# One loop over 64 graphs for four graph layers, with the directed layers taken upper, lower, single in a round

## The chip, the cores and the metric

The kernel runs on one core of one Trainium2 chip. The metric is the device time of one execution in microseconds. A core has TensorE (PE), VectorE (DVE), ScalarE (ACT), GpSimd (POOL) and SyncE (SP), which here issues all DMAs. Each engine runs its own list of instructions in order, and they meet at semaphores.

## The reference

For each of 64 independent graphs of 128 nodes, x is 128 x 384 and adj is 128 x 128. Four layers follow, each with a norm and a relu ahead of it and a residual sum behind it:

```python
h = relu(layernorm(x)); x = x + L0(h, adj)   # attention, 12 heads of 32, masked where adj is 0
h = relu(layernorm(x)); x = x + L1(h, adj)   # one directed layer
h = relu(layernorm(x)); x = x + L2(h, adj)   # two directed layers, the second on the output of the first
h = relu(layernorm(x)); x = x + L3(h, adj)   # attention, 12 heads, adj added to the scores, and an output projection
# a directed layer:
attn = softmax(h h^T / sqrt(D)) * adj;  attn = attn / (row sum + 1e-10)
ctx = upper(attn) @ (h Wl + bl) + diag(attn) * (h Ws + bs) + lower(attn) @ (h Wr + br)
out = relu(layernorm(ctx) * gain + offset)
```

To keep precision with 16-bit products, each operand of a product is held as a high and a low half in fp16 (hi, lo), and each product is three matmuls (`three_products`, L147).

## The kernel before

The kernel runs four phases one after the other. x of all 64 graphs stays in SBUF between them. `attention` (L347) serves L0 and L3, `directed` (L923) serves L1 and L2; in L2 the tasks of the first and the second directed layer of neighbouring graphs alternate. Within a phase a software pipeline is written out by hand in `step`: on each engine the list of operations of one task, each for the graph that is k tasks ahead or behind. `Phase.run` (L103) and `TwoLayerPhase.run` (L129) repeat it. Between two phases the engines meet, the next layer's weights are scaled, turned by TensorE where needed and split into halves by ScalarE and VectorE (`find_scales` L264, `split_high` L292, `split_low` L285, `turn` L301). Their loads and part of the search for their largest value (`largest`, L231) are done in the phase before.

In attention a task is: norm (`norm` L479, `normed` L534), turn h on TensorE (`turn_h` L798) and split it (`turned_hi` L540, `turned_lo` L650), project q and k (`project_turned` L807) and v (`project_v` L819), scores (`score` L829), the bias added and the row maximum found by VectorE, four heads at a time (`biased_max` L655), exponentials by ScalarE into f32 (`exponents` L545). TensorE then turns the f32 probabilities, 12 tiles of 128 x 128 (`turn_probs` L838), ScalarE takes the high half out of PSUM (`p_split` L570, the instruction at L572) and VectorE the low half (`p_split` L689, instruction at L692), and TensorE multiplies by v (`attend` L844). In L3 the result is turned (`turn_o` L855) and projected (`project_out` L862); GpSimd sums the scores to find rows that are all zero (`fold_scores` L501).

In a directed task TensorE computes h h^T (`similarity` L1294), the left, right and own projection (`project` L1301), turns the masked exponentials (L1311) and combines (L1335 to L1338, the last of these products waits for `right_lo` of GpSimd). VectorE has the row maximum, mask, diagonal, the sums with biases (`biased` L1197), the low half of the left values (`left_lo` L1193, instruction at L1195), `context` (L1202) and its statistics. GpSimd computes the power for the norm and the product behind it (`ctx_norm` L999, instructions L1003 and L1005), the low halves of the sides and of the right values (L1009, L1014), gain and offset (L1016, L1021). ScalarE has the exponential, the high halves, `norm_ctx` (L1088, instruction L1091) and `weighted_own` (L1081).

PSUM has eight banks. L0 and L3 use all of them, the directed phases seven.

## Time and profile before

| | us |
|---|---|
| median of 3 runs (lowest, highest) | 2752.17 (2751.03, 2753.88) |
| the profiled execution | 2754.08 |
| its span, first to last instruction | 2752.5 |
| TensorE busy | 2520.6, 92% |
| VectorE busy | 2336.4, 85% |
| ScalarE busy | 1804.1, 66% |
| GpSimd busy | 1453.0, 53% |
| DMA, mean over the span | 60.19 MB, 22 GB/s |
| mean granted clock of TensorE, as a share of full speed | 0.979 |

In 40 slices of 68.8 us, busy tenths, with the clock below them (9 is 90% or more):

```profile
PE   5999999986999999699999999999969999999998
...
DVE  5778777776999999688888888888859999999997
...
PEclk9999999997999999799999999999979999999998
```

The first nine slices are L0, the next seven L1, then thirteen of L2, and the last eleven L3; the dips are the changes of phase. Busy times of matmuls overlap, since a product's modelled end lies beyond the start of its successor: what a product costs is read from start to start.

### The profile page before, as it was taken

To read this page: it belongs to the slowest core of one execution; us is meant where nothing else is said; L and a number is where in the kernel's file an instruction comes from. 1 tells how busy PE (TensorE), PEld (TensorE's weight loads), DVE (VectorE), ACT (ScalarE), POOL (GpSimd) and SP (SyncE) were. 2 spreads that over 40 slices of the span, in tenths; PEclk is the share of its full clock that TensorE was granted. 3 is DMA by queue.
4 is the path that set the end of the run, shared out by engine and by line. 5 is a ranking of instruction groups with operands and counts; after the bars stand their busy time and mean duration, and the time that the engine had idled before them with its cause. 6 is when DMAs were issued, how large, how long until landed. Compare 5 with 4: busy or idle time off the path is not lost. (4 is left out here: it accounts for less than half of the span.)

```text
span 2752.5 us, 86859 instructions
## 1 busy us (share of the span) xinstructions
PE 2520.6 (92%) x27969; PEld 1884.4 (68%) x27969; DVE 2336.4 (85%) x9515; ACT 1804.1 (66%) x4409; POOL 1453.0 (53%) x2016
## 2 busy tenths in 40 slices
PE   5999999986999999699999999999969999999998
PEld 4888888874666665466666666666648888888886
DVE  5778777776999999688888888888859999999997
ACT  5888888874555555455555555555538777777775
POOL 1233232324777777477777777777734434444443
PEclk9999999997999999799999999999979999999998
DMA  3011010102000000100000000000000000000000
GB/s 105 28 30 29 28 30 27 30 14 88 9 9 10 10 10 9 46 10 10 10 10 10 10 10 10 10 10 10 10 6 22 24 25 23 27 23 27 23 27 23
DMA packets 73988, 60.19 MB, mean 22 GB/s; under 512 B 7888, under 2 KB 73936, under 8 KB 73936
## 3 DMA queue, kind: packets, MB, share of 16 engines
q1 hardware_dynamic: 73936, 59.54, 7.1%
q8 instruction: 27, 0.44, 0.1%
q14 instruction: 25, 0.20, 0.0%
HBM read 46.92 MB, written 12.58 MB: 22 GB/s over the span
## 5 line engine op out<-in xcount | busy, mean ns | idle before, releaser
L149 PE MATMUL bank<-L_w_hi,L_hT_hi 128*128 128x384 f16 x2112 | 691.7, 327 | 0.0
L151 PE MATMUL bank<-L_w_hi,L_hT_lo 128*128 128x384 f16 x2112 | 691.5, 327 | 0.0
L150 PE MATMUL bank<-L_w_lo,L_hT_hi 128*128 128x384 f16 x2112 | 691.4, 327 | 0.0
L550 ACT ACTIVATE raw_weights<-L_minus_scores,L_minus_max 128x128 f32<-128x128 f32 x1536 | 476.0, 389 | 69.5 <-DVE L_minus_max L665 67.7
L149 PE MATMUL bank<-L_hT_hi,L_w_hi 128*128 128x128 f16 x2304 | 413.4, 220 | 1.7 <-issue 1.2
L150 PE MATMUL bank<-L_hT_lo,L_w_hi 128*128 128x128 f16 x2304 | 413.3, 220 | 0.0
L151 PE MATMUL bank<-L_hT_hi,L_w_lo 128*128 128x128 f16 x2304 | 413.2, 220 | 0.0
L665 DVE CUSTOM_DVE_ANT_0 L_minus_scores<-bank,L_minus_score_bias 128x128 f32<-128x128 f32 x1536 | 347.8, 282 | 11.4 <-PE bank L834 5.9
L692 DVE TENSOR_TENSOR L_pT_lo<-bank,L_pT_hi 128x512 f16<-128x512 f32 x384 | 241.0, 682 | 126.6 <-ACT L_pT_hi L572 126.5
L1069 ACT ACTIVATE L_e<-bank,L_nmax 128x128 f32<-128x128 f32 x192 | 70.6, 368 | 365.6 <-DVE L_nmax L1154 365.6
L151 PEld LDWEIGHTS bank<-L_w_hi,L_hT_lo 128*128 128x128 f16 x2112 | 207.5, 98 | 138.2 <-issue 2.5
L483 POOL TENSOR_TENSOR L_ln_scale_bias<-L_var_eps,minus_half 128x1 f32<-128x1 f32 x128 | 70.5, 551 | 403.0 <-DVE L_var_eps L631 397.1
L150 PEld LDWEIGHTS bank<-L_w_lo,L_hT_hi 128*128 128x128 f16 x2112 | 207.5, 98 | 108.5 <-issue 2.2
L149 PEld LDWEIGHTS bank<-L_w_hi,L_hT_hi 128*128 128x128 f16 x2112 | 207.9, 98 | 98.7 <-issue 1.7
L491 POOL TENSOR_TENSOR L_xsum<-L_attended,L_bias_v 128x384 f32<-128x384 f32 x64 | 64.1, 1001 | 385.8 <-DVE L_attended L713 385.8
L1014 POOL TENSOR_TENSOR L_right_lo<-L_right,L_right_hi 128x384 f16<-128x384 f32 x192 | 211.3, 1101 | 75.6 <-ACT L_right_hi L1075 74.9
L1003 POOL TENSOR_TENSOR L_cln_scale_bias<-L_cvar_eps,minus_half 128x1 f32<-128x1 f32 x192 | 106.1, 552 | 235.1 <-DVE L_cvar_eps L1222 235.1
L149 PEld LDWEIGHTS bank<-L_hT_hi,L_w_hi 128*128 128x128 f16 x2304 | 227.1, 99 | 2.7 <-issue 2.5
L150 PEld LDWEIGHTS bank<-L_hT_lo,L_w_hi 128*128 128x128 f16 x2304 | 227.1, 99 | 0.7
L572 ACT ACTIVATE L_pT_hi<-bank 128x512 f16<-128x512 f32 x384 | 201.0, 596 | 40.4 <-PE bank L841 40.4
L151 PEld LDWEIGHTS bank<-L_hT_hi,L_w_lo 128*128 128x128 f16 x2304 | 227.1, 99 | 0.0
L1029 POOL TENSOR_TENSOR L_ob<-L_og,L_gain_offset_biases 128x384 f32<-128x384 f32 x192 | 191.4, 997 | 20.1 <-POOL L_og L1019 9.8
(165 smaller groups left out, 7531.3 us busy)
## 6 DMA issues: line engine op xcount, KB each, us to landing
adj_tile<-in_adj SPq DMA_DIRECT2D x320, 64.0 KB, 1.8
x<-in_x SPq DMA_DIRECT2D x64, 192.0 KB, 2.3
out<-L_result SPq DMA_DIRECT2D x64, 192.0 KB, 1.9
raw_weights<-in_L_gnn_Wq SPq DMA_DIRECT2D x2, 576.0 KB, 4.0
raw_weights<-in_L_gnn_Wk SPq DMA_DIRECT2D x2, 576.0 KB, 5.7
raw_weights<-in_L_gnn_Wv SPq DMA_DIRECT2D x2, 576.0 KB, 5.5
raw_weights<-in_L_gnn_Wl SPq DMA_DIRECT2D x2, 576.0 KB, 4.9
raw_weights<-in_L_gnn_Ws SPq DMA_DIRECT2D x2, 576.0 KB, 4.8
```

Of the source, the lines that this page charges most:

```text
L149: pe.matmul(out, stat[0], move[0], start=first, stop=False)
L150: pe.matmul(out, stat[0], move[1], start=False, stop=False)
L151: return pe.matmul(out, stat[1], move[0], start=False, stop=last)
L483: pool.tensor_tensor(ln[:, 0:1], ve[:, 0:1], minus_half[:, :], ALU.pow).then_inc(rstd_ready, 1)
L550: last = act.activation(probs[:, n_.slot(k), i, :], scores[:, i, :], ACT.Exp, bias=nmax[:, n_.slot(k), i:i + 1], scale=-1.0)
L572: act.activation(pT[0][:, HC * c:HC * c + HC, :], pT_banks[c][:, :].rearrange("p (h q) -> p h q", h=HC), ACT.Copy).then_inc(pT_hi[c], 1)
L665: last = dve.tensor_tensor_reduce(scores[:, i, :], s_banks[j][:, c128(c)], bias[:, n_.slot(), :], 1.0, -LOWEST, ALU.add, ALU.min, nmax[:, ...
L692: dve.tensor_tensor(pT[1][:, hs, :], pT_banks[c][:, :].rearrange("p (h q) -> p h q", h=HC), pT[0][:, hs, :], ALU.subtract).then_inc(pT_lo[ ...
L1003: pool.tensor_tensor(cln[:, 0:1], cve[:, 0:1], minus_half[:, :], ALU.pow).then_inc(d["crstd_ready"], 1)
L1014: pool.tensor_tensor(rightv[1][:, :], right[:, :], rightv[0][:, :], ALU.subtract).then_inc(d["r_lo"], 1)
L1029: pool.tensor_tensor(ob[:, :], og[:, :], tables[n_.kind(k)][1], ALU.add).then_inc(d["tail_ready"], 1)
L1069: act.activation(e[:, :], u_bank[:, 0:P], ACT.Exp, bias=nmax[:, 0:1], scale=scalev, accum_out=zsum[:, :]).then_inc(d["p_ready"], 1)
```

## The change

The four phases become one loop over rounds (`run_rounds`). A round holds one task of each of five kinds: `first` (L0), `single` (L1), `lower` and `upper` (first and second layer of L2) and `last` (L3), each for its own graph. A step is given as kind and lag: `n_.last(2)` in round n works on graph n - 2. `Order` says in which sequence tasks that share buffers follow each other: `first` and `last` share those of attention, and the directed kinds follow as upper, lower, single. x is kept for two graphs at each of four places (x0 to x3) and no longer for all. All weights live in SBUF at once; W0 is prepared first, and W1, W2 and W3 in a block before round 0 (`more_weights`), W2 and W3 loaded into the room that the raw W0 and W1 had, with three PSUM banks for turning instead of six. That room later holds f32 scratch tiles.

The probabilities are split in SBUF (`probs_hi` on ScalarE, `probs_lo` on VectorE) into `p16`, and a DMA turns both halves of four heads at once (`turn_probs` on SP, 128 x 1024 fp16, 256 KB); TensorE no longer turns them. All f32 transposes of h, of the masked exponentials and of the attended rows remain. The similarity, the masked exponentials and the turned h of a directed task now share one PSUM bank, left and right another, own and context a third; q, k, v, the turned h and the scores of attention share four, and the product with v, the turned attended rows and the output have the eighth bank. The arithmetic of each operation is unchanged. The core of the diff, with the indentation of nested functions taken off; the step lists of SP and ScalarE are left out:

```diff
+ATTENTION = Order(("first", 0), ("last", 2))
+DIRECTED = Order(("upper", 2), ("lower", 1), ("single", 0))
+NORMED = tuple(kind for kind in DIRECTED.kinds if kind != "upper")
+FIRST_ROUND, LAST_ROUND = -3, G - 1 + 4
+LOOP = (4 + 4) // 2 * 2, (G - 1 + -3) // 2 * 2
...
+def run_rounds(eng, step, before_round):
+
+    for n in range(FIRST_ROUND, LOOP[0]):
+        if n in before_round:
+            before_round[n](eng)
+        step(Round(eng, n))
+    with eng.Fori(LOOP[0] // 2, LOOP[1] // 2) as i:
+        values = {"i": i, "from": LOOP[0] // 2}
+        for s in (0, 1):
+            step(Round(eng, (2, s), values))
+    for n in range(LOOP[1], LAST_ROUND + 1):
+        step(Round(eng, n))
 
 
...
-                        def turn_probs(n_, k, c):
-                            wait(pe, probs_ready[c], n_.done(k))
-                            for j in range(HC):
-                                mm = pe.transpose(pT_banks[c][:, c128(j)], probs[:, n_.slot(k), HC * c + j, :], ident[:, :])
-                            mm.then_inc(pT_psum[c], 1)
...
+        dhT_bank, u_bank, e_bank = banks[0], banks[0], banks[0]
+        l_bank, r_bank = banks[1], banks[1]
+        own_bank, c_bank = banks[2], banks[2]
+        pv = banks[3][:, 0:H * (HD + 1)].rearrange("p (h e) -> p h e", h=H)
+        oT_bank, o_bank = banks[3], banks[3]
+        hT_bank, q_bank, k_bank, v_bank = banks[4], banks[5], banks[6], banks[7]
...
+def turn_probs(t, c):
+    if t is None:
+        return
+    wait_apart(sp, (pT_ready[c], t.count(-1, 16)), (p_lo[c], t.count()), (pv_psum, t.count(-1)))
+    sp.dma_start_transpose(pT[:, c, :, :],
+                           p16[:, c, :, :, :].rearrange("p a h n -> p (a h n)")).then_inc(pT_ready[c], 16)
...
+def more_weights(eng):
+    W0.ready(sp)
+    W1.ready(sp)
+    W2.load(sp)
+    W2.ready(sp)
+    W3.load(sp)
+    W3.ready(sp)
+
+load_x(Task(sp, ATTENTION, "first", 0, None))
+W0.load(sp)
+W1.load(sp)
+run_rounds(sp, step, {0: more_weights})
+sp.wait_ge(out_written, 16 * G)
+
+            @block.gpsimd
...
+def step(n_):
+    dir_norm(n_.single(0))
+    right_lo(n_.lower(1))
+    att_norm(n_.first(-1))
+    add_v_bias(n_.first(-1))
+    add_out_bias(n_.last(2))
+    fold_scores(n_.last(2))
+    context_norm(n_.lower(1))
+    fold_again(n_.last(2))
+    gain(n_.lower(1))
+    offset(n_.lower(1))
+    sides_lo(n_.single(0))
+    right_lo(n_.single(0))
+    context_norm(n_.single(0))
+    gain(n_.single(0))
+    offset(n_.single(0))
+    sides_lo(n_.upper(1))
+    right_lo(n_.upper(1))
+    dir_norm(n_.lower(0))
+    context_norm(n_.upper(1))
+    gain(n_.upper(1))
+    offset(n_.upper(1))
+    att_norm(n_.last(1))
+    add_attended(n_.first(-1))
+    sides_lo(n_.lower(0))
...
+def probs_hi(t, c):
+    if t is None:
+        return
+    wait_apart(act, (probs_ready[c], t.count()), (pT_ready[c], t.count(-1, 16)))
+    act.activation(p16[:, c, 0, :, :], probs[:, HC * c:HC * c + HC, :], ACT.Copy).then_inc(p_hi[c], 1)
...
+def dir_input(t):
+    if t is None:
+        return
+    if t.kind == "upper":
+        wait(act, d["hT_psum"], t.count(-1))
+        wait(act, d["tail_ready"], Task(act, DIRECTED, "lower", t.graph, t.values).count())
+        act.activation(dh[:, :], ob[:, :], ACT.Relu).then_inc(d["h2_ready"], 1)
+    else:
+        wait_apart(act, (d["ln_ready"], t.count(of=NORMED)), (d["hT_psum"], t.count(-1)))
+        x = x1 if t.kind == "single" else x2
+        act.activation(dh[:, :], x[:, t.parity(), :], ACT.Relu, bias=dln[:, 1:2],
+                       scale=dln[:, 0:1]).then_inc(d["h_ready"], 1)
...
+def probs_lo(t, c):
+    if t is None:
+        return
+    wait(dve, p_hi[c], t.count())
+    dve.tensor_tensor(p16[:, c, 1, :, :], probs[:, HC * c:HC * c + HC, :], p16[:, c, 0, :, :],
+                      ALU.subtract).then_inc(p_lo[c], 1)
...
+def add_to_x(t):
+    if t is None:
+        return
+    if t.kind == "upper":
+        wait(dve, xsum_ready, t.graph_count(-2))
+    wait(dve, d["tail_ready"], t.count())
+    old, new, ready = (x1, x2, x2_ready) if t.kind == "single" else (x2, x3, x3_ready)
+    dve.scalar_tensor_tensor(out=new[:, t.parity(), :], in0=ob[:, :], scalar=0.0, in1=old[:, t.parity(), :],
+                             op0=ALU.max, op1=ALU.add).then_inc(ready, 1)
...
+def step(n_):
+    dir_stats(n_.single(0))
+    dir_mean_var(n_.single(0))
+    dir_var_eps(n_.single(0))
+    att_var_eps(n_.first(-1))
+    left_lo(n_.lower(1))
+    dir_turned_lo(n_.single(0))
+    biased_max(n_.last(2), 0)
+    biased_max(n_.last(2), 1)
+    biased_max(n_.last(2), 2)
+    row_max(n_.single(0))
+    minus_row_max(n_.single(0))
+    context(n_.lower(1))
+    context_stats(n_.lower(1))
+    scaled_eps(n_.lower(1))
+    context_mean_var(n_.lower(1))
+    context_var_eps(n_.lower(1))
+    left_sum(n_.single(0))
+    mask(n_.single(0))
+    att_turned_lo(n_.first(-1))
+    part_sides(n_.single(0))
+    diagonal(n_.single(0))
+    v_lo_split(n_.last(2))
+    right_sum(n_.single(0))
+    probs_lo(n_.last(2), 1)
+    score_sums(n_.last(2))
+    left_lo(n_.single(0))
+    score_bias(n_.first(-1))
+    nonzero_sums(n_.last(2))
+    dir_turned_lo(n_.upper(1))
+    denominator(n_.single(0))
+    probs_lo(n_.last(2), 0)
+    probs_lo(n_.last(2), 2)
+    context(n_.single(0))
+    scaled_denominator(n_.single(0))
+    context_stats(n_.single(0))
+    scaled_eps(n_.single(0))
+    context_mean_var(n_.single(0))
+    row_max(n_.upper(1))
+    context_var_eps(n_.single(0))
+    minus_row_max(n_.upper(1))
+    biased_max(n_.first(-1), 0)
+    mask(n_.upper(1))
+    kept_rows(n_.last(2))
+    diagonal(n_.upper(1))
+    left_sum(n_.upper(1))
+    biased_max(n_.first(-1), 1)
+    denominator(n_.upper(1))
+    left_lo(n_.upper(1))
+    part_sides(n_.upper(1))
+    biased_max(n_.first(-1), 2)
+    right_sum(n_.upper(1))
+    add_to_x(n_.single(0))
+    dir_stats(n_.lower(0))
+    scaled_denominator(n_.upper(1))
+    row_sums(n_.last(2))
+    dir_mean_var(n_.lower(0))
+    row_scales(n_.last(2))
+    probs_lo(n_.first(-1), 0)
+    dir_var_eps(n_.lower(0))
+    attended_rows(n_.last(2))
+    context(n_.upper(1))
+    scaled_eps(n_.upper(1))
+    context_stats(n_.upper(1))
+    probs_lo(n_.first(-1), 2)
+    context_mean_var(n_.upper(1))
+    context_var_eps(n_.upper(1))
+    dir_turned_lo(n_.lower(0))
+    probs_lo(n_.first(-1), 1)
+    row_max(n_.lower(0))
+    turned_o_lo(n_.last(2))
+    minus_row_max(n_.lower(0))
+    v_lo_split(n_.first(-1))
+    left_sum(n_.lower(0))
+    add_to_x(n_.upper(1))
+    att_stats(n_.last(1))
+    att_mean_var(n_.last(1))
+    att_var_eps(n_.last(1))
+    add_result(n_.last(2))
+    att_stats(n_.first(-2))
+    mask(n_.lower(0))
+    drop_masked(n_.first(-2))
+    diagonal(n_.lower(0))
+    row_sums(n_.first(-1))
+    denominator(n_.lower(0))
+    row_scales(n_.first(-1))
+    attended_rows(n_.first(-1))
+    att_mean_var(n_.first(-2))
+    att_turned_lo(n_.last(1))
+    part_sides(n_.lower(0))
+    scaled_denominator(n_.lower(0))
+    right_sum(n_.lower(0))
+    score_bias(n_.last(1))
...
+def combine(t):
+    if t is None:
+        return
+    wait(pe, d["a_lo"], t.count())
+    wait(pe, d["l_lo"], t.count())
+    wait(pe, d["own_ready"], t.count())
+    three_products(pe, c_bank[:, 0:D], (sidesv[0][:, 0, :], sidesv[1][:, 0, :]),
+                   (leftv[0][:, :], leftv[1][:, :]), first=True, last=False)
+    wait(pe, d["r_hi"], t.count())
+    pe.matmul(c_bank[:, 0:D], sidesv[0][:, 1, :], rightv[0][:, :], start=False, stop=False)
+    pe.matmul(c_bank[:, 0:D], sidesv[1][:, 1, :], rightv[0][:, :], start=False, stop=False)
+    wait(pe, d["r_lo"], t.count())
+    pe.matmul(c_bank[:, 0:D], sidesv[0][:, 1, :], rightv[1][:, :], start=False, stop=True)\
+        .then_inc(d["c_psum"], 1)
...
+def step(n_):
+    project_q(n_.last(2))
+    dir_turn_h(n_.single(0))
+    score(n_.last(2))
+    combine(n_.lower(1))
+    similarity(n_.single(0))
+    project_left(n_.single(0))
+    att_turn_h(n_.first(-1))
+    project_v(n_.last(2))
+    project_self(n_.single(0))
+    turn_e(n_.single(0))
+    project_right(n_.single(0))
+    project_q(n_.first(-1))
+    dir_turn_h(n_.upper(1))
+    project_k(n_.first(-1))
+    combine(n_.single(0))
+    similarity(n_.upper(1))
+    score(n_.first(-1))
+    project_left(n_.upper(1))
+    project_self(n_.upper(1))
+    turn_e(n_.upper(1))
+    project_right(n_.upper(1))
+    attend(n_.last(2), 0)
+    attend(n_.last(2), 1)
+    attend(n_.last(2), 2)
+    combine(n_.upper(1))
+    project_v(n_.first(-1))
+    dir_turn_h(n_.lower(0))
+    turn_o(n_.last(2))
+    similarity(n_.lower(0))
+    project_left(n_.lower(0))
+    project_out(n_.last(2))
+    project_right(n_.lower(0))
+    attend(n_.first(-1), 0)
+    attend(n_.first(-1), 1)
+    attend(n_.first(-1), 2)
+    turn_e(n_.lower(0))
+    att_turn_h(n_.last(1))
+    project_self(n_.lower(0))
+    project_k(n_.last(1))
...
+
+pe.wait_ge(setup, 2)
+W0.ready(pe)
+run_rounds(pe, step, {0: more_weights})
```

## Rows read from the trace of the kernel before

**Rows 1.** The page, part 1: busy us, share, instructions.

```profile
PE 2520.6 (92%) x27969; PEld 1884.4 (68%) x27969; DVE 2336.4 (85%) x9515; ACT 1804.1 (66%) x4409; POOL 1453.0 (53%) x2016
```

**Rows 2.** Busy by stretch: length, busy us (instructions), granted clock, DMA share, GB/s.

```profile
200.00:300.00 100.00, 92.78 (x1584) 83.98 (x1584) 78.34 (x419) 83.91 (x221) 30.21 (x44) 1.00 0.10 29
800.00:900.00 100.00, 98.03 (x680) 60.96 (x679) 92.69 (x346) 57.73 (x130) 74.42 (x115) 1.00 0.03 9
1400.00:1500.00 100.00, 98.22 (x694) 61.82 (x693) 86.64 (x317) 57.30 (x132) 72.83 (x103) 1.00 0.03 10
2000.00:2100.00 100.00, 72.29 (x790) 56.74 (x789) 67.86 (x259) 52.33 (x122) 37.31 (x48) 0.85 0.04 11
2300.00:2400.00 100.00, 93.08 (x1409) 80.83 (x1410) 95.73 (x410) 77.29 (x199) 41.82 (x48) 1.00 0.07 24
```

**Rows 3.** Timeline, TensorE, one L3 graph: start, us, line, tiles, count.

```profile
2300.58 0.55 PE L859 MATMUL bank<-identity,L_attended 128*128 128x128 f32 x3 [0.60 <-DVE L_attended L713]
...
2303.98 0.33 PE L149 MATMUL bank<-L_w_hi,L_oT_hi 128*128 128x384 f16 x1
...
2305.44 1.47 PE L841 MATMUL bank<-identity,raw_weights 128*128 128x128 f32 x12
...
2306.75 0.33 PE L149 MATMUL bank<-L_w_hi,L_hT_hi 128*128 128x384 f16 x1
...
2309.59 0.95 PE L834 MATMUL bank<-L_kT,L_qT 32*128 32x128 f32 x24
...
2311.33 0.54 PE L859 MATMUL bank<-identity,L_attended 128*128 128x128 f32 x3 [0.79 <-DVE L_attended L713]
```

**Rows 4.** Timeline, several engines, in L2.

```profile
1505.85 0.34 PE L1338 MATMUL bank<-L_right_lo,L_sides_hi 128*128 128x384 f16 x1
...
1506.29 0.56 DVE L1207 TENSOR_TENSOR L_ctx<-bank,L_own_weighted 128x384 f32<-128x384 f32 x1 [0.81 <-PE bank L1338]
...
1509.65 0.55 POOL L1003 TENSOR_TENSOR L_cln_scale_bias<-L_cvar_eps,minus_half 128x1 f32<-128x1 f32 x1 [1.74 <-DVE L_cvar_eps L1222]
...
1510.05 0.56 DVE L1200 TENSOR_TENSOR L_right<-bank,L_gain_offset_biases 128x384 f32<-128x384 f32 x1
...
1510.42 0.67 POOL L1009 TENSOR_TENSOR L_sides_lo<-L_sides,L_sides_hi 128x256 f16<-128x256 f32 x1
...
1510.50 0.71 ACT L1091 ACTIVATE L_o<-L_ctx,L_cln_scale_bias 128x384 f32<-128x384 f32 x1 [0.16 <-POOL L_cln_scale_bias L1005]
...
1510.52 0.98 DVE L1195 TENSOR_TENSOR L_left_lo<-L_left,L_left_hi 128x384 f16<-128x384 f32 x1
...
1511.50 0.55 DVE L1133 BATCH_NORM_STATS2 L_bn<-x 128x6 f32 x1
...
1512.14 0.18 DVE L1137 BATCH_NORM_AGGREGATE L_mean_var<-L_bn 128x2 f32<-128x6 f32 x1
```

**Rows 5.** A group on VectorE by form: busy us, mean ns, idle before.

```profile
L665 DVE CUSTOM_DVE_ANT_0 L_minus_scores<-bank,L_minus_score_bias 128x128 f32<-128x128 f32 x1536 | 347.8, 282 | 11.4 <-PE bank L834 5.9 <-issue 5.5
```

**Rows 6.** Two single lines: duration ns, least, median, most.

```profile
L1195 DVE TENSOR_TENSOR L_left_lo<-L_left,L_left_hi x192: 544/910/1045, 661.2 to 2023.0; 128x384 f16<-128x384 f32 x192
...
L1160 DVE CUSTOM_DVE_ANT_0 L_e_masked<-L_e,adj_tile x192: 291/291/294, 656.9 to 2020.6; 128x128 f32<-128x128 f32 x192
```

**Rows 7.** The page, part 6: DMA issues, KB each, us to landing.

```profile
x<-in_x SPq DMA_DIRECT2D x64, 192.0 KB, 2.3
...
raw_weights<-in_L_gnn_Wk SPq DMA_DIRECT2D x2, 576.0 KB, 5.7
```

**Rows 8.** One line: first and last start of the L0 projections.

```profile
L812 PE MATMUL bank<-ones_in_rows_and,L_bias_rows x384: 219/219/314, 31.0 to 608.6; 128*128 128x128 f16 x192
```

**Rows 9.** Timeline, VectorE, preparing weights of L1 and L2.

```profile
642.94 0.17 DVE L269 TENSOR_SCALAR pow<-gall 128x4 int32<-128x4 int32 x1 [5.21 <-POOL gall L280]
...
1125.44 9.54 DVE L289 SCALAR_TENSOR_TENSOR L_w_lo<-bank,weight_scale,L_w_hi 128x384 f16<-128x384 f32 x18
```

**Rows 10.** DMA rate in 40 slices of 640 to 700 us.

```profile
GB/s 0 0 0 5 0 0 0 0 0 0 74 343 388 274 392 161 0 39 132 390 387 266 244 311 356 70 18 25 0 5 0 46 3 0 0 0 44 0 0 0
```

2023 lines of the change are left out of this document (969 added, 1054 removed).

## Prediction

> **What bounds the kernel now.** I read the page's engine totals first, then busy time by stretch, then one graph on TensorE in order of time, then the helpers' durations. TensorE is busy 92% of the span [rows 1]; in the directed stages 98% at full clock, in L3 93% beside a VectorE at 96%, in L0 93% [rows 2]. So TensorE's own work sets three stages and VectorE shares L3; the rest is the space between stages, where a stretch of 100 us holds only 72 us of TensorE work at clock 0.85 [rows 2].
>
> Time per graph follows from instruction counts. An L0 graph is 144 records, so 1584 records in 100 us are 11 graphs, 9.09 us each. A directed task is 47: 680 and 694 give 6.91 (L1) and 6.77, over the stretches 6.80 (L2). An L3 graph runs from turn to turn, 10.75 us here, 10.63 on the mean of its stretch (1409 records of 150) [rows 2, 3]. One graph therefore costs 9.09 + 6.91 + 2 x 6.80 + 10.63 = 40.2 us. 64 of them are 2575 us; 177 us of the 2752.5 us span are the start, three changes of stage and the end.
>
> **Part 1: work moved.** Of an L3 graph 0.79 us is idle and 1.31 us is the 12 transposes of probabilities [rows 3], so TensorE keeps 10.75 - 0.79 - 1.31 = 8.65 us. L0 is that without turning and projecting the output (0.38 + 1.46) and with six bias products more (0.34): 7.15. A directed task is 9 x 0.056 (similarity) + 34 x 0.1625 (nine products take 1.46 us) [rows 3] + 0.45 of transposes = 6.48. A round holds one task of each kind: 7.15 + 8.65 + 3 x 6.48 = 35.2 us of TensorE against 40.2 now. That is the most the change can win: 5 us a round, of which 2.6 are transposes and the rest idle time.
>
> VectorE: 2336 us [rows 1] less some 60 for weights and starts is 35.6 us a graph. About 2.5 of that is blocking behind GpSimd (below), so 33.1 us of bare work. ScalarE has 27.6, GpSimd 22.6 by the same division. The splits of probabilities stay (six of 512 columns on each of two engines) but read SBUF, not PSUM; the nearest row, 384 columns from SBUF, takes at least 0.544 us [rows 6], so 512 cost about 0.68 unblocked, which is what the split costs now: no change.
>
> **Part 2: the order within a round.** TensorE has 35.2 us of work, VectorE 33 to 36. With both that full, every engine keeps a written order, and a chain that crosses engines is late wherever the next queue is behind. I follow the cycle that closes on itself from one round to the next, with handovers of the trace. (a) VectorE's stats of x1 for the single layer to its turn on TensorE: stats 0.64 to the aggregate, 0.25, 0.30, GpSimd's power and product 0.85 up to ScalarE's start, ScalarE 0.76: 2.8 [rows 4]. (b) From that turn TensorE's own work to the end of project_k(first) is 12.9: turns 3 x 0.34 and 0.11, score 0.95, combine 0.98, similarity 0.5, left, v and right 1.46 each, self 1.63, q and k of first 30 x 0.056 = 1.68 each; two short waits (the scaled q; the upper layer's input, behind ScalarE's third block of exponentials) add 0.2 and 0.5: 13.6. (c) combine(single) and the handover: 0.98 + 0.28 = 1.3 (VectorE starts 0.44 after the last product) [rows 4]. (d) VectorE from context(single) to dir_var_eps(lower): 7 operations of 384 columns that follow each other at 0.48 [rows 4], 3 blocks of score maxima at 0.86 (four heads of 0.21) [rows 5], one 512-column split 0.62, part_sides 0.36, two masks 0.46, row_max 0.28, some 14 tiny ones at 0.12: 9.4. (e) GpSimd 0.85, ScalarE 0.76 and its queue 0.25: 1.85. (f) Turn of the lower layer, its two halves evicted, up to similarity: 0.34 + 0.2 + 0.52 + 0.6 = 1.65. (g) TensorE to turn_e(lower): 0.5 + 3 x 1.46 + attend 1.05 (2.84 up to the scores less 1.46 and 0.33) [rows 3] + 0.11 = 6.05. (combine(upper) waits up to 1.8 us for right_lo, with project_v(first) and all of TensorE behind it, but the cycle through VectorE is later.) (h) Waiting 0.45 for the last layer's input (x3 comes from combine(upper) over nine handovers), then the turn and its two halves: 2.0. (i) VectorE's last four operations: 1.2. Unblocked sum 39.85.
>
> Blocking: one half-split starts at 1510.52 while GpSimd works from 1510.42 to 1511.09, and takes 0.98 instead of 0.544; the line's median is 0.910 [rows 4, 6]. The trace has no round in which GpSimd's order stands beside these operations, so its price has two ends: zero, and 0.5 for each of two such splits in (d), left_lo(upper) and probs_lo(first). I take the line's median excess, 0.37 each, 0.75: the period is 40.6 us.
>
> **Part 3: the DMA transposes.** Six a round, 256 KB each, from SP's queue; what is queued behind one is the next transposes, adjacency loads and the write. No transpose by DMA is in the trace. Nearest rows: a plain 192 KB lands in 2.3 us, 576 KB in 5.7 [rows 7], so 256 KB plain would be about 2.7. Between probs_lo(first, 1) and attend(first, 1) my round leaves 4.7 us, so up to there it is hidden; lower bound of its cost nothing, upper (three times the plain time) 3.3 us a round. I take nothing, the end the plain rows are nearest to. The Trainium skill, "DMA: Bandwidth & Descriptors", Latency and other measured facts, gives an effective 261 GB/s for a DMA transpose, an estimated 1.0 us for 256 KB on top of the fixed part; by that the sum stays, and no row here shows it.
>
> **Part 4: outside the full rounds.** All five tasks run in rounds 2 to 62, 61 rounds. Start: first L0 projection at 31 us [rows 8], 30 here (one x load less before the weights), then graph 0 alone through attention with latencies bare: about 22. Weights of W1, W2, W3 in one lump before round 0, nothing beside it: 16 reductions of 1.34 = 21; three scales, each with 5.2 us of waiting for GpSimd's maximum [rows 9] and 1.8 of small steps = 21; 39 splits, now at 0.53 each (9.54 for 18) [rows 9], with three banks for six about 0.67 = 26; loads of W2 and W3 bare, 5.5 and 2.8 MB at the 350 to 390 GB/s of such loads [rows 10] plus fixed parts = 26; bias rows, first pieces and the value bias 9: 103. Rounds 0 and 1 are half empty but bound by the chain: 31 and 35. Rounds 63, 64, 65 and the last write: 34 + 31 + 22 = 87. Together 30 + 22 + 103 + 31 + 35 + 87 = 308 us, where the kernel before has 177. TensorE idles in the lump; the clock after it is the 0.85 kind of stretch, at most 10 us and in those numbers.
>
> **Sum.** 308 + 61 x 40.6 = 2785 us of span. The profiled execution took 2754.08 with a span of 2752.5, and the median of the runs is 2752.17: the difference is under 0.1%, so the forecast is 2785 us. The point of no change is a period of (2752.5 - 308)/61 = 40.07.
>
> **Rivals.** First, that the queues fit. If the waits of (b), (e), (h) and the blocking vanish, because engines shift against each other until the idle time lies where it is harmless, the period is 40.6 - 0.7 - 0.25 - 0.45 - 0.75 = 38.45 and the time 308 + 61 x 38.5 = 2656 us. For it: VectorE has 5 us of idle time a round, mostly ahead of the single layer's scores, and L3 runs today at 96% VectorE. Against: (d) follows combine(single) and (g) follows (f) without a free place. It decides the sign below 40.07.
>
> Second, that transposes land late: at 8 us each, attend(first) waits 3.3 us, period 43.9, 2986 us. It bites above 4.7 us. For it: the plain time is already 2.7 and three are issued closely; against: other queues are nearly empty.
>
> Third, that every VectorE operation with two SBUF operands is blocked by GpSimd, not only the half-splits: then mask, diagonal and add_to_x in (d) pay 0.37 each too, period 41.7, 2852 us. For it: GpSimd will be busy 22.6 us of each round of 40. Against: mask never took over 294 ns in 192 [rows 6], though in the order of before it rarely meets GpSimd. The Trainium skill, "SBUF — State Buffer", states that the shared port pair is an exclusive lock for a VectorE operation with two SBUF inputs against a GpSimd operation that reads SBUF; by that rule the sum would be this rival's.
>
> Fourth, that the single loop doesn't overlap layers at all in some rounds; the counts in the code rule it out, and I give it nothing.
>
> **How the numbers follow.** Forecast 2785 (its own range, periods 40.2 to 41.3: 2760 to 2827) 0.36; queues fit 0.33; two-operand blocking 0.15; late transposes 0.11; the edge between the first two, periods within 0.1 of 40.07, 0.05. Faster by over 0.2% 0.33, slower by over 0.2% 0.61, within 0.2% 0.06 (the edge and a sliver of the forecast); 0.2% is about what a measurement can tell here. The range is 2620 to 2910: below it lies a third of the fitting queues (0.11), above it most of the late transposes (0.08).
>
> **What would show it.** Right: records per 100 us in mid-kernel giving a round of 40 to 41 us; TensorE busy 86 to 88% there with waits at combine(upper) and dir_turn_h(lower); the first full round not before 210 us; VectorE's probs_lo at a mean of 0.8 to 1.1 us. Wrong: a wait of attend for a DMA; mask or add_to_x above 0.35 and 0.6 us; a lump of weights far from 100 us; a TensorE clock below 1.00 in full rounds, which I assume stays where it was at 93% busy [rows 2].

## Result: slower, 3006 us for 2753

The changed kernel takes 3006.3 us (median, 3003.3 to 3006.8) beside 2752.8 us for the kernel before on the same chip: a ratio of 1.092, interval 1.090 to 1.094. The forecast was 2785 us, its range 2620 to 2910. The sign was right; the size was not, and the time lies 96 us above the range. The profiled execution has a span of 3004.7 us.

The page of the changed kernel: engine totals, busy tenths of TensorE and VectorE in 40 slices of 75 us, granted clock, instruction queues, and the groups that matter.

```profile
span 3004.7 us, 83638 instructions
...
PE 2456.4 (82%) x26433; PEld 1745.5 (58%) x26433; DVE 2378.9 (79%) x9515; ACT 1792.9 (60%) x4406; POOL 1452.8 (48%) x2010
...
PE   2378988888888888888888888888888888889885
...
DVE  4558888777887887888788788778878878878984
...
PEclk8689999999999999999999999999999999999997
...
q8 instruction: 272, 4.46, 0.7%
q14 instruction: 171, 1.40, 0.2%
...
L181 PE MATMUL bank<-hT_hi,w_hi 128*128 128x128 f16 x2304 | 436.3, 227 | 102.1 <-issue 100.8
...
pT<-p SPq DMA_TRANSPOSE x384, 2.8
```

Against [rows 1] TensorE does 1536 products fewer and is busy 64 us less, at 82% for 92%. One line, the products of the attention's projections, has 100.8 us of idle time put down to "issue", the time in which an engine waited for nothing that the profile shows; before, TensorE had 1.7 us of it in all.

TensorE's waits in the changed kernel, total, times and longest:

```profile
PE bank L181 <- issue: 100.8, 25, 4.9
PE bank L181 <- ACT raw_weights L810: 80.5, 63, 2.3
PE bank L1410 <- ACT raw_weights L764: 60.7, 87, 3.9
PE bank L181 <- DVE dir_hT_lo L1054: 58.1, 66, 1.3
```

25 times: the loop holds rounds 8 to 59, two to a turn, so it jumps back 25 times. The starts of one instruction that each round has once (fold_scores on GpSimd) give the length of every round. Rounds that are written out take 41.1 to 41.6 us. From the first jump on they alternate: 48.4, 41.8, 47.2, 41.6, 47.1, 41.6, and so on to the last turn, and behind the loop 41.4, 41.4, 41.1 again.

One jump on TensorE, VectorE and ScalarE:

```profile
1535.84 0.22 PE L183 MATMUL bank<-hT_hi,w_lo 128*128 128x128 f16 x1
1540.21 0.26 PE L181 MATMUL bank<-hT_hi,w_hi 128*128 128x128 f16 x1 [4.16 <-issue]
1540.27 0.31 PE L182 MATMUL bank<-hT_lo,w_hi 128*128 128x128 f16 x1
1540.38 0.31 PE L183 MATMUL bank<-hT_hi,w_lo 128*128 128x128 f16 x1
...
1537.40 0.56 DVE L1034 BATCH_NORM_STATS2 dbn<-x 128x6 f32<-128x384 f32 x1 [2.25 <-issue]
...
1539.97 0.71 ACT L764 ACTIVATE raw_weights<-x,dln_scale_bias 128x384 f32<-128x384 f32 x1 [2.82 <-issue]
```

The same place as stretches (us, busy us and count of each engine, then granted clock, DMA share, GB/s):

```profile
1535.84:1540.20 4.36, 0.22 (x4) 0.06 (x2) 1.59 (x7) 1.54 (x4) 1.47 (x3) 0.80 0.31 81
1540.20:1542.20 2.00, 1.99 (x20) 2.00 (x21) 0.00 (x0) 0.47 (x1) 1.88 (x4) 0.50 0.03 8
1542.20:1544.20 2.00, 1.71 (x17) 1.34 (x15) 0.00 (x0) 0.77 (x2) 1.32 (x2) 0.50 0.00 0
1544.20:1550.00 5.80, 5.80 (x59) 4.20 (x60) 4.51 (x29) 4.13 (x12) 1.51 (x1) 0.91 0.01 3
```

TensorE stands for 4.16 us, VectorE for 2.25, ScalarE for 2.82. Then TensorE's products come 0.107 us apart in the place of 0.056: the granted clock is 0.50, the lower of its two levels (1.2 and 2.4 GHz), for the four us behind the wait, and the 0.91 of the stretch after them holds about one more. At half speed these 5 us lose 2.5. A jump costs the standing and what the lower clock takes behind it.

### The profile page after: what moved, and what is told of

It is laid out like the page before. It is cut to its first block and busy times, and to the rows that moved or that the text cites. A ratio compares the mean times of both kernels' runs of the same rounds, so it can differ in the third digit from the quotient of the medians.

```text
span 3004.7 us, 83638 instructions
## 1 busy us (share of the span) xinstructions
PE 2456.4 (82%) x26433; PEld 1745.5 (58%) x26433; DVE 2378.9 (79%) x9515; ACT 1792.9 (60%) x4406; POOL 1452.8 (48%) x2010
## 3 DMA queue, kind: packets, MB, share of 16 engines
q8 instruction: 272, 4.46, 0.7%
## 5 line engine op out<-in xcount | busy, mean ns | idle before, releaser
L181 PE MATMUL bank<-w_hi,dir_hT_hi 128*128 128x384 f16 x1728 | 568.1, 329 | 2.1 <-DVE raw_weights L1122 2.1
L182 PE MATMUL bank<-w_lo,dir_hT_hi 128*128 128x384 f16 x1728 | 567.4, 328 | 0.0
L183 PE MATMUL bank<-w_hi,dir_hT_lo 128*128 128x384 f16 x1728 | 567.1, 328 | 0.0
L730 ACT ACTIVATE probs<-minus_scores,minus_max 128x128 f32<-128x128 f32 x1536 | 473.9, 387 | 78.6 <-DVE minus_max L947 78.6
L181 PE MATMUL bank<-hT_hi,w_hi 128*128 128x128 f16 x2304 | 436.3, 227 | 102.1 <-issue 100.8
L183 PE MATMUL bank<-hT_hi,w_lo 128*128 128x128 f16 x2304 | 437.8, 227 | 0.0
L182 PE MATMUL bank<-hT_lo,w_hi 128*128 128x128 f16 x2304 | 437.4, 227 | 0.0
L947 DVE CUSTOM_DVE_ANT_0 minus_scores<-bank,minus_score_bias 128x128 f32<-128x128 f32 x1536 | 342.8, 285 | 40.2 <-PE bank L1362 31.9
L955 DVE TENSOR_TENSOR p<-probs,p 128x512 f16<-128x512 f32 x384 | 265.2, 704 | 3.0 <-ACT p L737 2.9
L737 ACT ACTIVATE p<-probs 128x512 f16<-128x512 f32 x384 | 237.0, 618 | 0.5
```

The lines of the kernel that those rows point to most:

```text
L181: pe.matmul(out, stat[0], move[0], start=first, stop=False)
L182: pe.matmul(out, stat[0], move[1], start=False, stop=False)
L183: return pe.matmul(out, stat[1], move[0], start=False, stop=last)
L730: last = act.activation(probs[:, i, :], scores[:, i, :], ACT.Exp, bias=nmax[:, t.slot(), i:i + 1], scale=-1.0)
L737: act.activation(p16[:, c, 0, :, :], probs[:, HC * c:HC * c + HC, :], ACT.Copy).then_inc(p_hi[c], 1)
L947: last = dve.tensor_tensor_reduce(scores[:, i, :], s_banks[j][:, c128(c)], bias[:, t.slot(), :], 1.0, -LOWEST, ALU.add, ALU.min, nmax[:, t ...
```

## Experiments

What was open after the two traces: whether the jump is the cause or only marks every second round; what its cost goes by; and whether the period of 41.1 us is set by the cycle that the forecast walked round, or by something that a better order removes. Each variant was executed once, the one marked as timed four times; the kernel before, executed beside them, took 2752 to 2755 us. A difference of a few us between two variants is therefore not told apart from chance here. The variants without a loop have line numbers two lower than the changed kernel; the one with added work has its own.

**1. No loop at all.**

```
-    with eng.Fori(LOOP[0] // 2, LOOP[1] // 2) as i:
-        values = {"i": i, "from": LOOP[0] // 2}
-        for s in (0, 1):
-            step(Round(eng, (2, s), values))
+    for n in range(*LOOP):
+        step(Round(eng, n))
```

> The changed kernel with rounds 8 to 59 written out one behind another too, so that no engine has a loop; nothing else differs. In the trace of the changed kernel the rounds written out take 41.1 to 41.6 us each, but 25 of the rounds in the loop take about 47.2 us, every second one. Theory J (the jump back to the head of the loop's long body costs some 5.5 us each time): all rounds 41.1 to 41.6 us, no idle time of 4 us put down to issue on TensorE, granted clock 1.00 all the way, and 3005 - 25 x 5.5 = 2868 us (2855 to 2885). Rival P (it is the parity of the round: a buffer or a DMA of every second graph): every second round still takes 47 us, and the time stays at 3005. Rival F (fresh instructions cost the same wherever they lie, the loop only shows it): the rounds get longer than 41.6 us throughout, and the time lies between 2900 and 3005.

Measured 2856.6 us: 149.7 less, 6.0 for each of the 25 jumps, of which TensorE's standing is 4.0 on average, and the 2.0 left fit the lower clock behind it. The rounds have a median of 41.1 and a mean of 41.3 us, the alternation is gone, TensorE's waits for issue are 0.2 us in all, and the clock from 1000 to 2000 us is 1.00:

```profile
1000.00:2000.00 1000.00, 886.02 (x9948) 631.59 (x9949) 888.51 (x3556) 663.55 (x1642) 534.05 (x750) 1.00 0.26 58
```

The jump is the cause; parity falls. The 1.00 is rounded: in the 61 full rounds the clock still fell five times, for 3.4 us each. Fresh code in a straight line costs little: some rounds are 0.3 to 1.7 us longer than the shortest, with small issue waits on VectorE.

**2. Four rounds to a turn.**

```
-    with eng.Fori(LOOP[0] // 2, LOOP[1] // 2) as i:
+    with eng.Fori(LOOP[0] // 4, LOOP[1] // 4) as i:
...
-        for s in (0, 1):
-            step(Round(eng, (2, s), values))
+        for s in (0, 1, 2, 3):
+            step(Round(eng, (4, s), values))
```

> The changed kernel with four rounds to a turn of the loop in the place of two: 13 turns and 12 jumps back for 26 and 25. Theory J at the same cost for each jump: one round in four long, 12 x 5.5 = 66 us above the version without a loop, 2934 us (2920 to 2950). A rival of J by size (what is fetched at a jump grows with the body, twice as long now): a jump costs 10 us or more, and the time stays near 3000. Rival P: every second round long, 3005 us.

Measured 2915.8 us, 59.2 above the straight version over 12 jumps: 4.9 each. One round in four is long (44.5 to 46.4 us). TensorE stands 36.6 us in 12 waits:

```profile
PE bank L181 <- issue: 36.6, 12, 3.5
```

A body twice as long does not make a jump dearer (3.05 us of standing in the place of 4.03). That is theory J, at a price a little under the expected one (2915.8 us, where the range began at 2920).

**3. The kernel before without its loops** (both of its loop forms written out, as in 1), executed once and then timed.

> The kernel before with all of its loops written out (its loop bodies hold two tasks of one layer each, in the place of two whole rounds of four layers). Its trace shows tasks of equal length in its loops and 1.7 us of TensorE idle time put down to issue in all, so theory J says that its jumps cost nothing: 2752 us, within 8 us. If every jump costs something whatever the body's size, of its 160 or so jumps even 0.3 us each would bring 50 us: 2700. If fresh code costs more than code run again, it gets slower, 2770 or more.

> The kernel before with all of its loops written out, once more and timed in three rounds: one execution gave 2720.3 us beside 2754.8. If that stands, 2718 to 2723 us, a ratio of 0.987 to 0.989, faster than both kernels of this case; if it was chance, 0.995 to 1.005.

The first execution gave 2720.3 us, the timing 2718.5 (2717.4 to 2719.9) beside 2753.0: 0.987, interval 0.986 to 0.989. I had expected no change, and that was wrong: writing out its 142 short jumps (28, 26, 60 and 28) saves 34.5 us together, 0.24 each, though TensorE shows next to no wait for issue. This version beats both kernels of the case.

**4. The kernel before with longer bodies.**

```
-        for t in range(self.first):
+        start = (G - self.last) // 2 * 2 - (G - self.last - self.first) // 6 * 6
+        for t in range(start):
             step(Turn(eng, self, t))
-        with eng.Fori(self.first // 2, (G - self.last) // 2) as i:
+        with eng.Fori(0, (G - self.last - self.first) // 6) as i:
             values = {"i": i}
-            for s in (0, 1):
-                step(Turn(eng, self, (2, s), values))
+            for s in range(6):
+                step(Turn(eng, self, (6, start + s), values))
```

> The kernel before with six tasks to a turn of the loop in the place of two in its layers L0, L1 and L3 (8 jumps back in each in the place of 28, 26 and 28; L2 with its 60 jumps stays). It tells what the cost of a jump goes by. Written out, this kernel gained 34.5 us over 142 jumps, 0.24 us each; in the changed kernel a jump costs 5.9 us (148 us over 25), with four rounds to a turn 4.9 (59 over 12). On TensorE a body holds about 290 products in L0 before, 870 here, 780 in the changed kernel. If the cost comes with the body's length, L0's and L3's 16 jumps cost some 4 to 6 us each here, and the gain from the fewer short jumps is 58 x 0.24 = 14 us: 2752 + 64 to 96 - 14 = 2800 to 2835 us, with idle times of some 4 us on TensorE put down to issue. If it comes with something else in the changed kernel (the number of queues busy, the DMA transposes in flight), the jumps stay cheap: 2738 us (2730 to 2745).

Measured 2839.1 us, 86 above the kernel before and 4 above the expected range:

```profile
PE bank L835 <- issue: 58.3, 16, 4.2
```

Exactly 16 waits, the 8 jumps of L0 (864 products in the body) and the 8 of L3 (900), 3.6 us each. The 8 jumps of L1, whose body of six small tasks holds some 280 products, show none. With the 14 us that the fewer short jumps save, the 16 long ones cost about 100 us, 6.3 each. So the price of a jump goes by the length of what is jumped over, not by the merged kernel: up to some 300 products on TensorE it was 0.24 us, at 822 and more (two rounds of the changed kernel are 822) it is 4.9 to 6.3. Where between the two it changes was not tried, and since the lists of all engines grow together, the runs do not tell which engine's length counts.

The queues that bring instructions (q8 and q14 of the page) fit this. In the kernel before they moved 27 and 25 packets in all and none between 300 and 400 us, in the loop of L0:

```profile
q8 instruction: 27, 0.44, 0.1%
q14 instruction: 25, 0.20, 0.0%
```

Written out it moved 223 and 182, in that stretch 13 and 7; with six tasks to a turn 192 and 78. The Trainium skill, "Runtime: NRT & Kernel Launch", Instruction fetch mechanics, says that a taken branch to an instruction outside the two pages at hand has to wait until that page is fetched, and gives this as one reason why kernels prefer written-out code. The runs agree with that rule, which gives no price; it stood in no rival of the forecast.

**5. The cycle itself.** In the straight version the seven steps of the forecast can be read off one round:

```profile
1465.87 0.55 DVE L1032 BATCH_NORM_STATS2 dbn<-x 128x6 f32<-128x384 f32 x1
...
1468.86 0.52 PE L1408 MATMUL bank<-identity,raw_weights 128*128 128x128 f32 x3 [0.50 <-ACT raw_weights L762]
...
1482.60 0.33 PE L179 MATMUL bank<-left_hi,sides_hi 128*128 128x384 f16 x1
...
1483.87 0.56 DVE L1141 TENSOR_TENSOR raw_weights<-bank,raw_weights 128x384 f32<-128x384 f32 x1
...
1494.17 0.55 POOL L601 TENSOR_TENSOR dln_scale_bias<-dvar_eps,minus_half 128x1 f32<-128x1 f32 x1 [0.85 <-DVE dvar_eps L1046]
...
1495.93 0.52 PE L1408 MATMUL bank<-identity,raw_weights 128*128 128x128 f32 x3 [0.75 <-ACT raw_weights L762]
...
1497.70 0.23 PE L179 MATMUL bank<-dir_hT_hi 128*128 128x128 f16 x1 [0.93 <-DVE dir_hT_lo L1052]
...
1506.99 0.55 DVE L1032 BATCH_NORM_STATS2 dbn<-x 128x6 f32<-128x384 f32 x1
```

These are stats(single), its turn, combine(single), context(single), the norm of lower, its turn, its similarity, and the next round's stats(single): 2.99, 13.74, 1.27, 10.30, 1.76, 1.77 and 9.29 us, 41.12 together.

Three kernels test whether this loop of handovers holds the period. Each is the straight version with one edit; `extra` is two more bn_stats of 128 x 384 that nobody reads.

```
ScalarE
+                    weighted_own(n_.upper(1))
                     left_hi(n_.upper(1))
                     exponents(n_.first(-1), 0)
                     sides_hi(n_.upper(1))
                     probs_hi(n_.first(-1), 0)
-                    weighted_own(n_.upper(1))
TensorE
+                    project_v(n_.first(-1))
                     combine(n_.upper(1))
-                    project_v(n_.first(-1))
VectorE
+                    extra(n_.single(0))
                     add_to_x(n_.single(0))
```

> The version without a loop with one edit on ScalarE: weighted_own of upper ahead of left_hi of upper and of the exponents of head group 0, in the place of behind them. TensorE waits 1.16 us per round for it at combine of upper (80.0 us in 63 waits), the longest group of waits but one. If waits of TensorE add up, the period falls by 0.5 to 1.1 us (the operands of sides come next, at 0.5 us less) and the time to 2790 to 2825. If the chain to dir_turn_h of lower sets the period, the wait there grows by what is saved here, the period stays at 41.1 and the time at 2857 (2845 to 2870). I expect the second.

> The version without a loop with one edit on TensorE: project_v of first (9 products, 1.46 us) goes ahead of combine of upper, so it fills the 1.16 + 0.36 us that TensorE waits there. If waits of TensorE add up, the period falls by 1.2 to 1.5 us: 2757 to 2780. If the chain from VectorE's context of single to dir_turn_h of lower sets the period, TensorE only comes to that wait earlier: it grows from 0.75 to about 2.2 us, the period stays at 41.1, and the time at 2857 (2845 to 2870). I expect the second.

> The changed kernel without a loop (2856.6 us, 41.1 us a round) with work added: two more bn_stats of 128x384 on VectorE in every round (about 0.47 us apart, 0.95 us together; their result is read by nobody), directly ahead of add_to_x of single, in the stretch from context of single to dir_var_eps of lower. VectorE's busy time is then 36.9 of 41.1 us. Theory of the cycle (this stretch of VectorE's queue lies on the loop that sets the period, since dir_turn_h of lower waits 0.75 us for its end): the whole 0.95 us comes out, period 42.0 to 42.2 us, about 64 x 0.95 = 61 us: 2917 us (2905 to 2930). Rival (VectorE still has slack in the stretch, as its share of 81 to 89 per cent would have it): less than 0.3 us a round, 2857 to 2875.

ScalarE's edit: 2853.8 us, period 41.1 unchanged. The wait that it removes (80.0 us) comes back as 59.7 us at the next operand, sides_lo, and the wait at dir_turn_h stays (87.7 us for 88.1). TensorE's edit: 2903.0 us, period 42.1 at the median. Only one round, at the end, is shorter than 41.0, and at dir_turn_h(lower) TensorE waits 2.02 us for 0.75:

```profile
PE bank L1408 <- ACT raw_weights L762: 170.0, 128, 3.9
```

Both say that a wait saved on TensorE ahead of that turn is worth nothing: from turn(upper) to turn(lower) it is 15.36 us at the median in the straight version and in both. TensorE's edit is even 46 us slower, which I had not expected: the part behind the turn, up to the next turn(single), takes 15.09 us for 14.06. That is the lower clock behind the longer wait (0.96 from 1000 to 2000 us): in 19 rounds in the middle without a fall of the clock in this part it takes 14.06 us as before, in 36 with one 15.27. That project_v now waits for the bank of scores (43.6 us for 11.2) comes ahead of the turn and costs nothing.

Work added to VectorE's stretch: 3012.8 us, +156, where I expected +61. All of it came out, and more:

```profile
1524.14 0.54 DVE L1169 BATCH_NORM_STATS2 extra_stats<-gain_offset_biases 128x6 f32<-128x384 f32 x1
1524.60 0.53 DVE L1170 BATCH_NORM_STATS2 extra_stats<-gain_offset_biases 128x6 f32<-128x384 f32 x1
1525.06 1.17 DVE L1179 SCALAR_TENSOR_TENSOR x<-raw_weights,x 128x384 f32<-128x384 f32 x1
...
1529.97 0.52 PE L1417 MATMUL bank<-identity,raw_weights 128*128 128x128 f32 x3 [2.30 <-ACT raw_weights L763]
...
1531.74 0.29 PE L179 MATMUL bank<-dir_hT_hi 128*128 128x128 f16 x1 [0.93 <-DVE dir_hT_lo L1053]
1531.83 0.31 PE L180 MATMUL bank<-dir_hT_lo,dir_hT_hi 128*128 128x128 f16 x1
1531.93 0.31 PE L181 MATMUL bank<-dir_hT_hi,dir_hT_lo 128*128 128x128 f16 x1
```

The two operations take 0.92. They push add_to_x onto GpSimd's right_lo (from 1524.90), and it takes 1.17 for 0.54: blocking of the kind that the forecast priced. So 1.55 us reach TensorE's wait (2.30 for 0.75), and behind a wait of that length its products come 0.10 us apart, not 0.056, again the lower clock level. The period is 43.8 us at the median, 2.7 more for 0.92 us of work: turn(upper) to turn(lower) takes 16.90 us for 15.36, and the part behind it 15.20 for 14.06. So what is added to this stretch of the cycle comes out in the period, and more than its own length. That a shorter stretch would give a shorter period is not shown by it.

**6. Shortening the cycle.** First VectorE alone, then VectorE and ScalarE, then the four queues of VectorE, ScalarE, TensorE and GpSimd, twice. Each edit moves many lines; what is shown is the part of each that bears on what follows. The first, e4_add_early, on VectorE (biased_max(first, 2) and what follows in its list also move):

```
                     biased_max(n_.first(-1), 1)
+                    part_sides(n_.upper(1))
+                    add_to_x(n_.single(0))
-                    denominator(n_.upper(1))
                     left_lo(n_.upper(1))
-                    part_sides(n_.upper(1))
-                    biased_max(n_.first(-1), 2)
+                    dir_stats(n_.lower(0))
+                    denominator(n_.upper(1))
                     right_sum(n_.upper(1))
-                    add_to_x(n_.single(0))
-                    dir_stats(n_.lower(0))
```

> The version without a loop, with one more edit on VectorE: in the straight rounds of the changed kernel add_to_x of single starts 2.06 us after its input is there (offset of single ends at 2794.65, add_to_x starts at 2796.71), behind biased_max of first and right_sum of upper. Here add_to_x of single, the statistics of lower behind it, and part_sides of upper go ahead of them. Theory of the cycle (the chain context of single, tail, add_to_x, norm of lower, its turned input sets the period by the waits of 0.75 us at dir_turn_h of lower and 0.93 at similarity): dir_input of lower 1.5 to 2 us earlier, period 0.6 to 0.9 us shorter than without this edit, about 67 x 0.75 = 50 us: 2818 us (2805 to 2840). Rival (the wait of 1.27 us at combine of upper, for weighted_own on ScalarE, comes before it in TensorE's order and nothing of it is touched; the time gained there is lost at the next wait): period unchanged, 2868 us, or slower where biased_max of first is now late for the exponents.

The second, e5_chain, on ScalarE (weighted_own and VectorE's list move too):

```
                     exponents(n_.first(-1), 2)
+                    dir_input(n_.lower(0))
+                    probs_hi(n_.first(-1), 2)
+                    dir_turned_hi(n_.lower(0))
                     exponents(n_.first(-1), 1)
-                    probs_hi(n_.first(-1), 2)
-                    dir_input(n_.lower(0))
-                    probs_hi(n_.first(-1), 1)
-                    dir_turned_hi(n_.lower(0))
                     norm_context(n_.upper(1))
+                    probs_hi(n_.first(-1), 1)
                     turned_o_hi(n_.last(2))
```

> The version without a loop (2856.6 us, 41.1 us in most rounds) with the whole chain from single's tail to lower's turned input moved forward on both queues that it runs through. The look at the edit on VectorE alone (2893.7 us) showed why that gained nothing: dir_input of lower began at 1513.6 in its round though its norm needed only 1512.5, behind two groups of exponents and a half of probs on ScalarE, TensorE's wait at dir_turn_h of lower was 1.30 us in the place of 0.75, and the time saved at combine of upper was lost there. Here VectorE has part_sides and right_sum of upper, add_to_x of single and dir_var_eps of lower all ahead of biased_max 2 of first, and ScalarE has weighted_own of upper ahead of the exponents of head group 0, dir_input of lower between the exponents of groups 2 and 1, dir_turned_hi of lower ahead of those of group 1. Theory of the cycle: waits at combine of upper from 1.5 to 0.7 us or less, at dir_turn_h of lower from 0.75 to 0.2, period from 41.1 to 39.3 to 40.2 us, time 2735 to 2800, about 2775. Rival (each time gained in one place is lost in the next, since other chains, such as the attention's scores to exponents to transposes, are as long): 41.0 to 41.4 us, 2850 to 2900.

The third, e8_all, on TensorE and GpSimd (the lists of VectorE and ScalarE move too):

```
                     combine(n_.upper(1))
-                    project_v(n_.first(-1))
                     dir_turn_h(n_.lower(0))
+                    project_v(n_.first(-1))
                     turn_o(n_.last(2))
...
+                    dir_norm(n_.lower(0))
                     right_lo(n_.upper(1))
-                    dir_norm(n_.lower(0))
```

> The version without a loop with its queues reordered along the whole cycle. The trace of e5_chain had the stretch from dir_turn_h of upper to dir_turn_h of lower at 14.57 us in the place of 15.36 (the chain did come forward by 0.8), but the rest of the round grew by 2.6, since turned_o_hi stood behind the exponents of group 1 on ScalarE: TensorE's wait at project_out 1.54 us, then 0.50 and 0.68 behind it. Here turned_o_hi goes ahead of those exponents; dir_stats of lower directly behind left_lo of upper; dir_norm of lower ahead of right_lo of upper on GpSimd; dir_input of lower ahead of the exponents of group 2; TensorE does combine of upper, dir_turn_h of lower and only then project_v of first, so that its 1.46 us fill the wait of 0.93 for the turned input; add_result of last goes ahead of att_mean_var of last (wait of 0.36 at attend); dir_input of upper ahead of left_hi of single (wait of 0.46). Theory of the cycle: from dir_turn_h of upper to similarity of lower 17.1 down to 15.4 us, the rest down by 0.4 to 0.8: period 38.6 to 39.8 us, 2695 to 2775 us. Rival (gain in one place, loss in the next): 41 us and more, 2850 to 2900.

The fourth, e9_all2, on ScalarE as against the third (three more operations move):

```
                     probs_hi(n_.first(-1), 2)
+                    exponents(n_.first(-1), 1)
                     turned_o_hi(n_.last(2))
+                    probs_hi(n_.first(-1), 1)
                     norm_context(n_.upper(1))
-                    exponents(n_.first(-1), 1)
-                    probs_hi(n_.first(-1), 1)
```

> The kernel e8_all with three places mended. In its trace the stretch from dir_turn_h of upper to similarity of lower was 16.14 us in the place of 17.13, but VectorE then waited 2.40 us at probs_lo 1 of first, since probs_hi 1 stood behind the exponents of group 1 and those behind norm_context of upper on ScalarE; TensorE waited 2.48 us at project_right of lower behind that, and its next nine products came 0.32 us apart in the place of 0.16, 1.4 us more. Here ScalarE does the exponents of group 1 and turned_o_hi, probs_hi 1 ahead of norm_context of upper, sides_hi of upper goes ahead of the exponents of group 0, VectorE does left_sum of lower ahead of v_lo_split of first, and probs_lo 2 of last goes behind minus_row_max of upper, so that context of single starts 0.5 us earlier. Theory of the cycle: 11.6 us from dir_turn_h of single to that of upper, 15.7 to 16.1 to similarity of lower, 11.9 to 12.3 to the next dir_turn_h of single: period 39.2 to 40.0 us, 2730 to 2790 us. Rival (gain in one place, loss in the next): 41 us and more, 2850 and more.

Measured 2893.7, 2973.8, 2985.2 and 3029.4 us: all slower than 2856.6, and in all four my forecast for them was wrong. The periods are 41.4, 43.1, 43.3 and 44.1 us at the median. From turn(upper) to turn(lower) the straight version takes 15.36 us, up to similarity(lower) 17.14, and from turn(lower) to the next turn(single) 14.06. In the first edit VectorE's part, context(single) to dir_var_eps(lower), came down from 10.01 to 8.74 us, yet turn(lower) came later, at 15.86: ScalarE still had the lower layer's input behind exponents and a half of the probabilities. In the second and third the stretch did get shorter (14.57 us to the turn; 13.64, and 16.15 to the similarity), but the rest of the round grew, to 16.75 and 18.14 us, because an operation that I had moved back met its reader elsewhere: turned_o_hi behind exponents (TensorE 1.54 us at project_out), then probs_hi behind norm_context. In the fourth the stretch up to the similarity is longer again (18.05 us). The third, in one round:

```profile
1519.27 0.78 DVE L953 TENSOR_TENSOR p<-probs,p 128x512 f16<-128x512 f32 x1 [2.40 <-ACT p L735]
...
1521.04 0.35 PE L179 MATMUL bank<-w_hi,dir_hT_hi 128*128 128x384 f16 x1 [2.48 <-DVE raw_weights L1120]
1521.21 0.50 PE L180 MATMUL bank<-w_lo,dir_hT_hi 128*128 128x384 f16 x1
1521.51 0.53 PE L181 MATMUL bank<-w_hi,dir_hT_lo 128*128 128x384 f16 x1
1521.83 0.53 PE L179 MATMUL bank<-w_hi,dir_hT_hi 128*128 128x384 f16 x1
```

The 2.40 us on VectorE become 2.48 on TensorE, and the nine products behind come 0.32 us apart for 0.16, at a granted clock of 0.54. So none of four edits by hand, of many lines each, improved the order on record. Whether some other order of the queues reaches a period of 39 us is open; these runs neither show nor exclude it.

## Why the prediction was right and wrong

The whole miss can be laid out in spans. Forecast 2785; the loop's jumps +150 (3004.7 - 2854.9); the period +43 (61 rounds at a mean of 41.3 for 40.6); outside the full rounds +27. Together 3005, measured 3004.7. Without the jumps the time would have been 2857 us, inside the range but above the 2760 to 2827 that the forecast gave itself.

**The step that failed** is the sum itself, 308 + 61 x 40.6: it lets every full round cost the same, whether its code is written out or looped, and so puts the 25 jumps back at nothing without giving a reason. The runs show 150 us for them, 6.0 each. None of the four rivals was about it. The rows of the kernel before gave no warning: its directed stages, looped too, run at 98% [rows 2], but over bodies of at most 300 products, and the new body has 822. No row gave a price for that; a term bounded from nothing up would have been due, with the count of 25 jumps beside it.

**Part 1, work moved:** right. The forecast gave TensorE 35.2 us of work a round; it is busy 36.6 in the straight version (0.886 of 41.3). It gave VectorE 33.1 bare and 35.6 with its blocking; it is busy 36.7 (0.889 of 41.3).

**Part 2, the cycle:** the path is right and the size nearly, in one step by luck. Steps (a) to (f) were forecast at 2.8, 13.6, 1.3, 10.15 with blocking, 1.85 and 1.65, and (g) to (i) together at 9.25; the list in 5 has 2.99, 13.74, 1.27, 10.30, 1.76, 1.77 and 9.29. Sum 40.6 for 41.12. No step is off by over 0.2 us; between 41.1, the median round, and the mean of 41.3 lie the longer rounds of fresh code. The luck is in (d): the 0.75 us of blocking that it counts were put on left_lo(upper) and probs_lo(first), and in the straight version these take 0.545 and 0.684 us in every full round, as they do unblocked. What does fall on GpSimd there is denominator(upper), an operation of 128 x 1, which takes 0.85 us at the median where denominator(single) takes 0.14. The waits stand where the forecast said, at combine(upper) (80.5 us) and dir_turn_h (60.7 us).

**Part 3, the transposes:** right. They land in 2.8 us for 2.7 forecast, and in all 384 the attention waited 9.3 us for one, in three waits, one when the pipeline starts (2.6) and two when it runs empty (6.1 and 0.5). The Trainium skill, "DMA: Bandwidth & Descriptors", Latency and other measured facts, made it an estimated 1.0 us plus a fixed part; 2.8 does not contradict that, and no row here separates the two parts.

**Part 4, outside the full rounds:** 335 for 308 in the span of the straight version. The start to the first turn took 33 us for 30; graph 0's attention 21 for 22 (33.43 to 54.87); the lump of weights 93 for 103 (to 147.4); rounds 0 and 1 78 for 66; the end 110 for 87. Half-empty rounds were mis-sized: rounds 63 and 64 take 41.5 and 41.4 us like full ones, for the same chain goes through them, where I had 34 and 31 for rounds 63 and 64.

**Rivals.** Queues fit: no full round of the changed or the straight kernel took under 41.0 us. Late transposes: gone with 2.8 us. Two-operand blocking: not as a price on every such operation, for mask has a mean of 281 ns, add_to_x 551 ns in the changed kernel, and probs_lo 704 ns, below the 0.8 to 1.1 that I gave. But the order of the queues puts the same few operations beside GpSimd in nearly every round. One round of the straight version, left_lo(lower), diagonal(single) and denominator(upper), each with what GpSimd does:

```profile
1509.00 0.91 POOL L625 TENSOR_TENSOR right_lo<-raw_weights,right_hi 128x384 f16<-128x384 f32 x1
1509.10 1.23 DVE L1126 TENSOR_TENSOR left_lo<-raw_weights,left_hi 128x384 f16<-128x384 f32 x1 [0.81 <-ACT left_hi L786]
...
1518.50 1.00 POOL L632 TENSOR_TENSOR raw_weights<-raw_weights,gain_offset_biases 128x384 f32<-128x384 f32 x1
1518.54 1.11 DVE L1082 CUSTOM_DVE_ANT_0 raw_weights<-raw_weights,identity 128x128 f32<-128x128 f32 x1
...
1529.70 1.00 POOL L642 TENSOR_TENSOR raw_weights<-raw_weights,gain_offset_biases 128x384 f32<-128x384 f32 x1
1529.86 0.85 DVE L1089 SCALAR_TENSOR_TENSOR den<-zsum,tsum 128x1 f32<-128x1 f32 x1
```

Their like in rounds without such a meeting take 0.55, 0.29 and 0.14; the means of these three over the rounds in the middle are 1.21, 1.04 and 0.80. Only the last lies in (d). In the first edit of 6, which moves it, it takes 0.17 on average, and probs_lo(first, 0) 0.94 for 0.68 in its place. The rule of the Trainium skill, "SBUF — State Buffer", Who interferes with whom, of a lock that VectorE and GpSimd share, agrees with these meetings: each of the three begins after GpSimd's operation and outlasts it. What it is worth depends on which operations meet, and that has to be walked through in the order of both queues.

**What would show it wrong** named a clock below 1.00 in full rounds, and that came: 0.95 to 0.98 in the looped stretches. It follows from the jumps, as experiment 1 shows with 1.00 (0.997 unrounded).

Of the 252 us between the two spans, then, 150 are jumps. The rest is the exchange that the forecast described: 61 rounds at 41.3 are 2519 us where 64 graphs took 2575, 56 less, and outside them stand 335 us for 177, 158 more: 102 together, as measured (2854.9 - 2752.5).

## What to carry to other kernels

Before merging loops into one, count the jumps and the products in the body: a jump over a long body cost 5 to 6 us here, a short one 0.24, and writing the loop out took it away (2753 to 2718 us for the kernel before). In a software pipeline over several engines, follow the cycle that closes on itself by its handovers: it gave the period to 2%, with some luck in one step, and two waits removed on TensorE ahead of where the cycle enters gained nothing. Place each blocked operation by the order of both queues, not by what was blocked in another order. Reordering by hand to shorten the cycle moves operations off other readers' time: look at each moved operation's reader in the trace before trusting a sum.
